# A halved last expert step, halved first rows of the attention, and 24 unread turns of the identity matrix on TensorE ahead of them

## The reference, cut to what matters

```python
x = x + tanh(g_xattn[0]) * mamba(ctx, layernorm(x))             # stage 1: state-space scan
x = x + tanh(g_ffn[0])   * moe(layernorm(x))                    # stage 2: 64 experts, 8 per token, 64 rows each
x = x + tanh(g_xattn[1]) * attention(layernorm(x), ctx, mask)   # stage 3: 16 heads, 4 batches of 256 rows
x = x + tanh(g_ffn[1])   * bitlinear_ffn(layernorm(x))          # stage 4: ternary weights, 1024 wide

def moe(x):       # x: (1024, 256)
    h = silu(inp @ wg) * (inp @ wu)          # per expert, inp: its rows of x
    out = h @ wd
    y = sum over a token's 8 experts of weight * out[expert, slot]
def attention(x, ctx):
    q = x @ Wq; k = ctx @ Wk; v = ctx @ Wv   # kernel: Wq and Wk folded into one matrix (mqk), Wv and Wo into another (nvo)
    p = softmax(q @ k.T / sqrt(128) + mask)
    return (p @ v) @ Wo
```

## Time and profile before

| what | value |
|---|---|
| runs before | 597.32, 597.74, 599.9 us; median 597.74 us |
| profiled execution, its own time | 596.96 us |
| its span | 594.7 us, 10156 instructions |
| PE busy | 483.3 us (81%) |
| DVE busy | 473.4 us (80%) |
| ACT busy | 363.1 us (61%) |
| POOL busy | 280.4 us (47%) |
| mean granted TensorE clock | 0.927 of full speed |
| chain of work that ended last, by engine | PE 33%, DVE 26%, issue 22%, ACT 8%, POOL 7% |

### The profile page before, as it was taken

One profiled execution on the slowest core, in us unless ns is written; L12 is line 12 of the kernel. 1 busy time (PEld: TensorE's weight loads), 2 busy tenths in 40 slices (PEclk: granted clock), 3 DMA queues, 4 the chain that ended last, 5 costly groups with the idle time before them and its releaser, 6 DMA issues.

```text
span 594.7 us, 10156 instructions
## 1 busy us (share of the span) xinstructions
PE 483.3 (81%) x3026; PEld 358.5 (60%) x3026; DVE 473.4 (80%) x1244; ACT 363.1 (61%) x828; POOL 280.4 (47%) x262
## 2 busy tenths in 40 slices
PE   6917777868769879899689999998789988998723
PEld 3302222322248746666489899997679977997602
DVE  4899999999886438888446865896898969875886
ACT  2785555536237646465646676678655796778543
POOL 3119777879210545550248548732786234333111
PEclk9957999879979989899879999999999999999856
DMA  5939300001004599996422103400234000000000
GB/s 159 230 66 339 89 1 0 1 1 35 1 15 137 173 259 296 299 287 193 149 68 69 28 4 75 65 2 2 33 57 72 2 2 2 19 2 0 1 18 18
DMA packets 45624, 48.60 MB, mean 82 GB/s; under 512 B 5660, under 2 KB 42118, under 8 KB 45574
## 3 DMA queue, kind: packets, MB, share of 16 engines
q1 hardware_dynamic: 41734, 36.46, 22.2%
q0 software_dynamic: 3840, 11.54, 8.6%
HBM read 41.43 MB, written 6.56 MB: 81 GB/s over the span
## 4 chain that ended last, share of the span: by engine, by line
PE 33%; DVE 26%; issue 22%; ACT 8%; POOL 7%; DMA 1%; DVEq 1%; SPq 0%; POOLq 0%; ACTq 0%
DVE hst L1753 7%; PE ps L1506 5%; PE ps L1449 4%; PE ps L1450 4%; PE ps L1451 4%; PE ps L1495 3%; PE ps L1371 2%; POOL dbu L518 2%; DVE hc L1762 2%; POOL G L597 2%; POOL pn L613 2%; PE ps L1268 1%; PE ps L1356 1%; PE ps L1406 1%; PE ps L1172 1%
## 5 line engine op out<-in xcount | busy, mean ns | idle before, releaser
L613 POOL TENSOR_TENSOR pn<-pr,pinv 128x512 f32<-128x512 f32 x64 | 67.6, 1058 | 92.8 <-DVE pinv L2147 92.3
L518 POOL TENSOR_TENSOR dbu<-du,brow 128x512 f32<-128x512 f32 x64 | 81.4, 1283 | 41.9 <-DVE du L1746 23.1
L1172 PE MATMUL ps<-hc,ident 128*128 128x512 f32 x128 | 75.2, 677 | 28.9 <-DVE hc L1762 27.5
L1753 DVE TENSOR_TENSOR_SCAN hst<-ps,dbu 128x512 f32<-128x512 f32 x64 | 77.9, 1217 | 0.2 <-POOL dbu L518 0.2
L756 ACT ACTIVATE ps<-dtv,amat 128x510 f32<-128x510 f32 x64 | 44.1, 690 | 49.6 <-DVE hst L1753 48.7
L914 ACT ACTIVATE pr<-ebuf,smin 128x256 f32<-128x256 f32 x128 | 63.8, 502 | 13.3 <-POOL pn L613 6.7
L1506 PE MATMUL ps<-pT,cS 128*128 128x256 f32 x256 | 66.5, 382 | 0.0
L575 POOL DMA_INDIRECT G<-token_rows,idx_x x32 | 39.8, 1245 | 50.4 <-DVE ebuf L2006 22.6
L1172 PEld LDWEIGHTS ps<-hc,ident 128*128 128x128 f32 x128 | 21.2, 202 | 68.5 <-DVE hc L1762 64.8
L597 POOL DMA_INDIRECT G<-expert_out,idx_g x48 | 51.0, 1063 | 11.6 <-issue 10.1
L1449 PE MATMUL ps<-xnT,mqk 128*128 128x256 f32 x128 | 47.4, 370 | 9.0 <-DVE qT L2113 5.0
(11 more groups left out here) (366 smaller groups left out, 1375.5 us busy)
## 6 DMA issues: line engine op xcount, KB each, us to landing
wdn<-in_L_ffn_wd SPq DMA_DIRECT2D x15, 384.0 KB
wgu<-in_L_ffn_wg SPq DMA_DIRECT2D x14, 384.0 KB
wgu<-in_L_ffn_wu SPq DMA_DIRECT2D x14, 384.0 KB
expert_out<-xn SPq DMA_DIRECT2D x11, 256.0 KB
wq<-in_L_xattn_Wq SPq DMA_DIRECT2D x2, 1024.0 KB, 9.2
wo<-in_L_xattn_Wo SPq DMA_DIRECT2D x1, 2048.0 KB, 15.7
wo<-in_L_ffn_w SPq DMA_DIRECT2D x2, 1024.0 KB, 6.9
expert_out<-pexp SPq DMA_DIRECT2D x5, 256.0 KB
```

The lines of the kernel that those rows point to most:

```text
L518: nc.gpsimd.tensor_tensor(dbu[:, j, :], du[:, j % 2, 512 * hb:512 * hb + 512], brow[:, j // 2, :], ALU.mult).then_inc(pool_dbu, 1)
L613: nc.gpsimd.tensor_tensor(pn[:, h % 2], pr[:, h % 2], pinv[:, h % 2, :].unsqueeze(2).to_broadcast([P, 2, L]), ALU.mult)\
L1172: pe.matmul(bank(2 + j % 2), ident[:], hc[:, j % 2, :], start=(isinstance(m, int) and m + k == 0), stop=(isinstance(m, int) and m + k == N ...
L1753: V.tensor_tensor_scan(hst[:, j, :], bank(j % 2), dbu[:, j, :], 0.0, ALU.mult, ALU.add)\
```

## The change

Four edits go together.

**The last expert step in halves.** For g = 15 ACT makes for each half q the copy and its high part one after the other, both straight from PSUM (`take_out_last`); DVE makes the low part of each half (`low_out_last`); `combine` waits for the second half only ahead of its second four matmuls. SP stores the results after both halves.

**Piece 2 of the ternary turns** moves ahead of the last `combine`.

**The first rows of the attention in halves.** For batch 0, `turn_xn3` writes its two halves to banks 2 and 3, each with a semaphore of its own; ACT and DVE split each half by itself; `queries(0,0)` starts with the first half. `queries(0,1)` writes to bank 5 rather than bank 0, and no longer waits till the first result has been read. ACT's `context_rows(0)` moves behind `q_high(0,0)`.

**The turns.** After the last ternary piece PE transposes `ident` against itself 24 times, into banks 4 and 5, with nothing that reads them.

```diff
+        def norm_out(b, j):
+            return ps[:, 2 + j, 0:L] if b == 0 else ps[:, 2, L * j:L * j + L]
+
+        def query_out(i):
+            return ps[:, 5 if i == 1 else 0, 0:L]
...
-                sp_.wait_ge(eo_ready, g + 1)
+                sp_.wait_ge(eo_ready, g + 1 if g < NG - 1 else NG + 1)
...
+            def take_out_last():
+
+                g = NG - 1
+                act.wait_ge(down_done, NG)
...
+                for q in range(2):
+                    found, share = ps[:, 4 + g % 2, H * q:H * q + H], slot_share[:, g % RING, q:q + 1]
+                    A(results[g % 3][:, q, :], found, ACT.Copy, scale=share).then_inc(eo_ready, 1)
+                    A(eo_hi[:, g % 2, q, :], found, ACT.Copy, scale=share).then_inc(eo_hi_ready, 1)
...
-            take_out(NG - 1)
+            take_out_last()
...
             def norm_high(b):
-                act.wait_ge(xnT3_in_psum, b + 1)
+                if b == 0:
+                    for j in range(2):
+                        act.wait_ge(xnT3_in_psum, j + 1)
+                        A(xnT3[0][:, 0, j, :], norm_out(0, j), ACT.Copy).then_inc(xnT3_hi, 1)
+                    return
+                act.wait_ge(xnT3_in_psum, b + 2)
...
             context_high(0)
-            context_rows(0)
             norm_high(0)
             q_high(0, 0)
+            context_rows(0)
             q_high(0, 1)
...
                 for q in range(2):
+                    if g == NG - 1 and q == 1:
+                        pe.wait_ge(eo_lo_ready, NG + 1)
...
+                if g == NG + 2:
+                    turn_ternary(2)
                 if 1 < g < NG + 2:
                     down(g - 2)
                 if g > 2:
                     combine(g - 3)
-            for k in range(2, 4):
-                turn_ternary(k)
+            turn_ternary(3)
+            for k in range(24):
+                pe.transpose(ps[:, 4 + k % 2, 0:P], ident[:], ident[:])
...
             def turn_xn3(b):
                 pe.wait_ge(xn3_ready, b + 1)
                 if b == 0:
-                    pe.wait_ge(wternT_ready, 4)
+                    pe.wait_ge(wternT_ready, 3)
...
-                        last = pe.transpose(ps[:, 2, L * j + P * cc:L * j + P * cc + P],
+                        last = pe.transpose(norm_out(b, j)[:, P * cc:P * cc + P],
                                             xn[:, cc, P * j:P * j + P], ident[:])
-                last.then_inc(xnT3_in_psum, 1)
+                    if b == 0 or j == 1:
+                        last.then_inc(xnT3_in_psum, 1)
...
-                wait_count(pe, q_ready, i)
+                    pe.wait_ge(wternT_ready, 4)
+                wait_count(pe, q_ready, (0, 0, 1)[i] if i < 3 else i)
                 for j in range(2):
-                    last = mm3(ps[:, 0, 0:L], [m[:, h, j, :] for m in mqk],
+                    if i == 0:
+                        pe.wait_ge(xnT3_ready, j + 1)
+                    last = mm3(query_out(i), [m[:, h, j, :] for m in mqk],
...
+            def low_out_last(q):
+
+                g = NG - 1
+                dve.wait_ge(eo_ready, NG + q)
+                dve.wait_ge(eo_hi_ready, NG + q)
+                V.tensor_tensor(eo_lo[:, g % 2, q, :], results[g % 3][:, q, :], eo_hi[:, g % 2, q, :].bitcast(F32),
+                                ALU.subtract).then_inc(eo_lo_ready, 1)
...
             def norm_low(b):
-                dve.wait_ge(xnT3_hi, b + 1)
+                if b == 0:
+                    for j in range(2):
+                        dve.wait_ge(xnT3_hi, j + 1)
+                        low(xnT3[1][:, 0, j, :], norm_out(0, j), xnT3[0][:, 0, j, :], xnT3_ready)
+                    return
```

More of the change, by code:

```diff
@@ L869, in take_out @@
                 A(eo_hi[:, g % 2], results[g % 3], ACT.Copy).then_inc(eo_hi_ready, 1)
+            def take_out_last():
+                g = NG - 1
+                act.wait_ge(down_done, NG)
+                act.wait_ge(hg_ready, NG)
+                act.wait_ge(d_eo[g % 3], 16 * (g // 3))
+                act.wait_ge(eo_lo_ready, g - 1)
+                act.wait_ge(summed, g)
+                for q in range(2):
+                    found, share = ps[:, 4 + g % 2, H * q:H * q + H], slot_share[:, g % RING, q:q + 1]
+                    A(results[g % 3][:, q, :], found, ACT.Copy, scale=share).then_inc(eo_ready, 1)
+                    A(eo_hi[:, g % 2, q, :], found, ACT.Copy, scale=share).then_inc(eo_hi_ready, 1)
             turn(0)
@@ L906, in q_high @@
                 wait_count(act, s_done, i - 1)
-                A(qT[0][:, h % 2], bank(0)[:, 0:L], ACT.Copy).then_inc(q_hi, 1)
+                A(qT[0][:, h % 2], query_out(i), ACT.Copy).then_inc(q_hi, 1)
             def exps(b, h):
@@ L1461, in turn_xn3 @@
                     for cc in range(2):
-                        last = pe.transpose(ps[:, 2, L * j + P * cc:L * j + P * cc + P],
+                        last = pe.transpose(norm_out(b, j)[:, P * cc:P * cc + P],
                                             xn[:, cc, P * j:P * j + P], ident[:])
-                last.then_inc(xnT3_in_psum, 1)
+                    if b == 0 or j == 1:
+                        last.then_inc(xnT3_in_psum, 1)
             def queries(b, h):
                 i = NH * b + h
-                if h == 0:
-                    pe.wait_ge(xnT3_ready, b + 1)
+                if h == 0 and b > 0:
+                    pe.wait_ge(xnT3_ready, b + 2)
                 if b == 0 and h == 0:
                     pe.wait_ge(mn_low, 4)
-                wait_count(pe, q_ready, i)
+                    pe.wait_ge(wternT_ready, 4)
+                wait_count(pe, q_ready, (0, 0, 1)[i] if i < 3 else i)
                 for j in range(2):
-                    last = mm3(ps[:, 0, 0:L], [m[:, h, j, :] for m in mqk],
+                    if i == 0:
+                        pe.wait_ge(xnT3_ready, j + 1)
+                    last = mm3(query_out(i), [m[:, h, j, :] for m in mqk],
                                [v[:, b % 2, j, :] for v in xnT3], j == 0, j == 1)
@@ L2059, in _ @@
                 placed(g)
-            low_out(NG - 1)
+            for q in range(2):
+                low_out_last(q)
             def hold(at):
@@ L2105, in norm3 @@
                 else:
-                    dve.wait_ge(xnT3_in_psum, b)
+                    dve.wait_ge(xnT3_in_psum, b + 1)
                 for cc in range(2):
@@ L2119, in norm_low @@
             def norm_low(b):
-                dve.wait_ge(xnT3_hi, b + 1)
+                if b == 0:
[3 more added lines that the diff above has]
+                    return
+                dve.wait_ge(xnT3_hi, b + 2)
                 low(xnT3[1][:, b % 2].rearrange("p a b -> p (a b)"), bank(2),
@@ L2128, in q_low @@
                 wait_count(dve, s_done, i - 1)
-                low(qT[1][:, h % 2], bank(0)[:, 0:L], qT[0][:, h % 2], q_ready)
+                low(qT[1][:, h % 2], query_out(i), qT[0][:, h % 2], q_ready)
             def masked(b, h):
```

## The result

The changed kernel takes 594.25 us (median of 8 runs, 592.38 to 595.68) against 597.87 for the kernel before in the same comparison. The ratio is 0.9934, with a 95% interval of 0.9914 to 0.9954. Between the medians that is a gain of 3.6 us in the one and 5.0 in the other; the ratios, which aren't the quotients of these medians, say 3.9 and 4.1. Forecast were 4.7, a ratio of 0.9921, which lies in both intervals. Both ratios are faster by more than the 0.5% that I took for the bound, though the upper ends of the intervals reach just past it. A few executions in the comparisons of e5 to e10, of the kernel before and of variants, took 649 to 2558 us and are left out of the ratios.

The account below looks back on a forecast made before the run. The prediction took the uncovered half-clock handover from stage 2 to stage 3 as the bound; gains of 0.34 + 2.08 + 1.44 + 0.86 = 4.7 us from the median 597.74 gave 593.0 us, range 591.5 to 595.4.

Parts of the forecast that it names:

- The chain as the bound: Uncovered half-clock handover, last expert step to POOL's first normalisation; gains there should reach the end whole, 4.7 us.
- Step 1: Last expert step: halved copies and subtractions plus the moved ternary piece let `add_experts` start 0.34 us earlier.
- step 3: Turn of the rows to end of first queries: halves at full clock take 2.29 us, a gain of 2.08.
- Step 4: End of first queries to scores: head 1's queries in bank 5 run during ACT's copy, gaining 1.44 us.
- 5, scores to exponentials: From the first scores to the exponentials: six matmuls in 0.98 us, exponentials at 2.05, a gain of 0.86 us.
- The signs: Expected profile: `add_experts` at 290.0, clock 1.00 from 290 to 310, POOL's first normalisation near 300.7 us.
- Step 2: 24 unread turns in PE's wait for the norm: cost 2.6 us, covered, gain nothing themselves but keep full clock.
- rival 2: Clock falls late, near 295.5, in waits around the rows: 1.4 us less gain, 594.4 us; chance 18%.
- The rule that spoke against step 2: Trainium skill's statement that full clock does not engage for transposes; by it the 24 turns would keep nothing, 594.7 us.
- rival 1: The turns don't hold the clock, rows still at 0.50: gain only 3.0 us, 594.7 us; chance 15%.
- Rival 3: Turns outlast the norm at 0.39 us each, ending 5.7 behind the rows' start: 598.7 us; chance 3%.

Follow-up runs that it names:

- e5: The changed kernel itself measured again, beside variants on one chip: 592.9 us, ratio 0.9931 to the kernel before; 14.9 us from last expert step to POOL's first normalisation.
- e10: e7 with 100 unread turns in the tail instead of 84: 590.93 us, ratio 0.9922 to the kernel before.
- e11: e6 with head 1's queries back in bank 0: handover 15.07 us, one profiled execution.
- e6: The changed kernel with 31 turns instead of 24 and six more between the rows' turns and the first queries: 593.6 us, ratio 0.9933 to the kernel before.
- e3: The changed kernel with head 1's queries back in bank 0, waiting till head 0's are read: handover 16.55 us, one execution.
- e2: The kernel before with only the 24 turns added behind the last ternary piece: 597.05 us against 598.24, ratio 0.9995.
- e4: The changed kernel with 60 turns instead of 24: handover 16.5 us, one execution.
- e1: The changed kernel without the 24 turns: 595.34 us against 598.24 for the kernel before, ratio 0.9952.
- e9: The kernel before, profiled once more with nothing changed: handover 18.9 us, one execution.
- e7: e6 with 84 more unread turns in the tail, behind the last matmuls into the hidden layer: 592.53 us, ratio 0.9921 to the kernel before.
- e8: The changed kernel with 12 turns instead of 24: handover 15.8 us, one execution.

## Why the prediction was right, and where it was not

**The chain as the bound: right.** Measured from one profile to the other, the handover fell by 4.84 us, and the rest behind it kept its 289.2 us, within the microsecond by which that rest scatters. Of the sum of 4.7, step by step, always from the rows above and the earlier trace rows:

| step | predicted | measured |
|---|---|---|
| 1, last expert step (to `add_experts`) | 0.34 | 3.60 - 3.11 = 0.49 |
| `add_experts` to the rows, unchanged | 0 | 4.06 - 4.05 = 0.01 |
| 3, rows to the end of the first queries | 2.08 | 4.37 - 2.39 = 1.98 |
| 4, to the scores | 1.44 | 2.38 - 0.93 = 1.45 |
| 5, scores to exponentials | 0.86 | 2.91 - 2.00 = 0.91 |
| sum | 4.7 | 4.84 |

Step 1 was set too small: `combine` began 1.81 after ACT's first copy rather than 1.95. The sixteen bf16 turns ahead of it held PE for 292.12 - 291.25 = 0.87, not 0.91, and it stood directly behind them, where I had left 0.1 between. In step 3 the first query came 1.46 behind the rows' turn, not 1.35; the rest of the step was as said. Step 4 bears the name of the bank and holds more than the bank: at a clock of 1.00 on both sides (e11 against e6) one bank costs 0.82 up to the scores and 1.2 up to POOL, so the rest of the 1.44 came with the clock.

The signs that I had named as times of the span came 3 to 4 us later than named (`add_experts` at 293.42, not 290.0; POOL at 304.16, not 300.7), as the last step itself began 3.56 later. Counted from that start they were met: 3.11 against 3.25, and 13.85 against 13.95.

**Step 2, the turns: right in mechanism and price, wrong in how sure the clock is.** 24 turns cost 2.79 us (2.6 predicted), under the cover of the norm. I gave the late fall (rival 2) 18%. It came in one of two profiles of the changed kernel, and in e3, which is the same kernel up to its fall: two of three. (e2 has the same 24 turns and a fall too, but behind a longer wait, 2.08 us.) Its price was said to be 1.4 us and was 1.1 (14.93 against 13.85): I had counted sixteen matmuls at 0.09 more each, and left out that PE waited 0.25 ahead of the scores at full clock, which the slower queries used up. The fall can stand between the forecast and the smaller gains measured; but with intervals of 1.2 to 1.6 us on each side of a ratio no run shows that it does, and e5, which has the fall in its profile, isn't slower than the first comparison or than e6.

**The rule that spoke against step 2: it doesn't hold here.** e4 has 6.9 us of turns alone at a clock of 1.00, in addition to the earlier trace rows, and 3.25 us without turns or other work lost the clock. Where the rule and these traces differ, the traces decide. So rival 1, which I had worked out as 3.0 us of gain, is not the case of the changed kernel. e1, which has no turns, comes out like it: 3.3.

**Rival 3: not met.** The turns end 1.07 before the rows; e4 shows that once they reach past the norm they delay the rows, at 0.11 each and not at the 0.39 of this rival.

**The range** (591.5 to 595.4) held, and faster was right. Its upper end doesn't follow from the 0.5 us named for it, which gives 594.5; the rest was added for rivals 1 and 2. That the forecast of 593.0 lies between the medians of the two comparisons (594.25 and 592.9) is partly luck of the scatter: the same kernel gave both.

## What to carry to other kernels

Where a chain of small steps hands over from one stage to the next, measure it by itself, from the last event ahead of it to the first behind it: here it repeats within 0.2 us where the clock does the same (e9; e6, e7 and e10), while the totals of ten runs can't tell one microsecond. Unread work on TensorE that fills a wait is worth what the following matmuls lose at half clock (1.55 us here), and only where the clock then holds. It held in all four profiles with the fill of e6 and in one of three with 24 turns; half the turns bought nothing in their one profile. Whether the next small waits must be filled too isn't shown: e4 and e11 held the clock across such waits. Shortening the chain itself gave twice as much as the clock (3.3 us, e1), and it gave that at half clock.

## What was unexpected of the hardware

- Turns of the identity matrix against itself, written and never read, keep the granted clock at 1.00: 60 of them for 6.7 us (e4), 0.11 us each.
- The clock fell after waits as short as 1.07 and 0.81 us with little work between (e5), and held in another execution of the same kernel with the same waits. Which of the two happens differed from run to run; what decides it stays open.
- 12 turns, ended 2.38 us before the rows, gave a handover of 15.8 us, against 15.4 without any (e8 and e1, one profile each).
- The last expert step begins anywhere between 285.5 and 290.7 us, and in two executions of the same changed kernel at 290.31 and 286.86. Part of it are falls of the clock in stage 2, such as one from 268.57 to 275.39 in e6 that other profiles don't have; what else is in it wasn't tried.
